# First chunk's mixing products in full fp32, W1 and W2 split later, and no identity products behind the first transposes

## What is computed

```python
t = rmsnorm(x, norm1_w)
xb = causal_depthwise_conv(t @ Wx, conv_w, conv_b)          # 4 taps along the sequence
r, i = sigmoid(xb @ Wa), sigmoid(xb @ Wi)
a = exp(-8 * softplus(lam) * r)
h = scan(a, sqrt(max(1 - a*a, 1e-12)) * (i * xb))            # h[s] = a[s] h[s-1] + b[s]
h1 = x + (h * gelu(t @ Wy)) @ Wo
u = rmsnorm(h1, norm2_w)
attn = h1 + (gelu(u @ Wg) * (u @ Wu)) @ Wd                   # Wg, Wu: 256 x 1024
x1 = layernorm(x + attn)
out = layernorm(x1 + relu(x1 @ W1 + b1) @ W2 + b2)           # W1: 256 x 1024
```

## Time and profile before

| | us |
|---|---|
| median of 3 runs | 622.78 (621.52 to 623.34) |
| the profiled execution | 621.15, of which the span is 619.4 |
| TensorE busy | 601.3 (97% of the span) |
| VectorE busy | 386.9 (62%) |
| ScalarE busy | 309.0 (50%) |
| GpSimd busy | 205.1 (33%) |

### The profile page before, as it was taken

The page is one execution under the profiler, slowest core; times in us unless marked ns, Lnnn a source line. Parts: engine busy times, 40 slices in busy tenths (PEclk is TensorE's granted clock), DMA queues, the critical chain, the costliest instruction groups (busy, mean ns, idle before and its releaser), DMA issues.

```text
span 619.4 us, 9569 instructions
## 1 busy us (share of the span) xinstructions
PE 601.3 (97%) x3681; PEld 536.6 (87%) x3681; DVE 386.9 (62%) x698; ACT 309.0 (50%) x580; POOL 205.1 (33%) x307
## 2 busy tenths in 40 slices
PE   7999988999999999999999999999999999999996
PEld 6897877789988898889888898888988898888996
DVE  5795676736585747747477465748467473663565
ACT  4865733365453754447444644537544473322353
POOL 5614137211724135130732216241451405241131
PEclk9999999999999999999999999999999999999999
DMA  8601001000100001010010101001000100000011
GB/s 274 228 2 34 1 2 35 0 1 2 34 1 1 34 1 36 2 34 1 1 35 2 34 1 35 0 1 35 2 1 1 35 1 1 1 19 18 0 35 35
DMA packets 13085, 15.69 MB, mean 25 GB/s; under 512 B 600, under 2 KB 12272, under 8 KB 13040
## 3 DMA queue, kind: packets, MB, share of 16 engines
q1 hardware_dynamic: 13040, 15.09, 7.2%
HBM read 10.89 MB, written 4.19 MB: 24 GB/s over the span
## 4 chain that ended last, share of the span: by engine, by line
PE 86%; DVE 8%; ACT 2%; POOL 2%; issue 1%; DMA 1%; POOLq 0%; DVEq 0%
PE psum L313 17%; PE psum L315 17%; PE psum L314 17%; PE psum L321 10%; PE psum L323 10%; PE psum L322 10%; PE psum L328 3%; DVE xb L847 1%; POOL normed L1218 1%; DVE row L922 1%; DVE xv L883 1%; DMA xs<-in_L_attn_x_dram 1%; PE psum L445 1%; PE psum L443 1%; PE psum L441 1%
## 5 line engine op out<-in xcount | busy, mean ns | idle before, releaser
L1247 POOL TENSOR_SCALAR gu_hi<-gu_raw 128x512 fp32r<-128x512 f32 x64 | 50.8, 794 | 318.3 <-DVE gu_raw L945 318.3
L955 DVE TENSOR_TENSOR hid_lo<-hid_raw,hid_hi 128x512 fp32r<-128x512 f32 x56 | 45.5, 813 | 83.9 <-ACT hid_hi L703 83.9
L699 ACT ACTIVATE hid_raw<-psum,vecs 128x512 f32<-128x512 f32 x56 | 38.4, 686 | 114.0 <-PE psum L315 114.0
L945 DVE TENSOR_TENSOR gu_raw<-psum,gu_raw 128x512 f32<-128x512 f32 x64 | 44.1, 689 | 81.3 <-PE psum L315 78.9
L321 PE MATMUL psum<-w_d_hi,gu_hi 128*128 128x256 f32 x256 | 72.8, 285 | 2.4 <-DVE gu_lo L950 2.4
L321 PE MATMUL psum<-w_hi,hid_hi 128*128 128x256 f32 x256 | 71.7, 280 | 0.6 <-DVE hid_lo L960 0.4
L323 PE MATMUL psum<-w_hi,hid_lo 128*128 128x256 f32 x256 | 71.8, 281 | 0.0
L323 PE MATMUL psum<-w_d_hi,gu_lo 128*128 128x256 f32 x256 | 71.8, 280 | 0.0
L322 PE MATMUL psum<-w_lo,hid_hi 128*128 128x256 f32 x256 | 71.7, 280 | 0.0
L322 PE MATMUL psum<-w_d_lo,gu_hi 128*128 128x256 f32 x256 | 71.6, 280 | 0.0
L690 ACT ACTIVATE gu_raw<-psum 128x512 f32<-128x512 f32 x64 | 38.1, 596 | 49.1 <-PE psum L315 48.4
(11 more groups left out here) (166 smaller groups left out, 1574.4 us busy)
## 6 DMA issues: line engine op xcount, KB each, us to landing
xs<-in_L_attn_x_dram SPq DMA_DIRECT2D x8, 512.0 KB, 3.5
out_dram<-row SPq DMA_DIRECT2D x15, 256.0 KB, 2.2
raw<-in_L_ffn_W_dram SPq DMA_DIRECT2D x2, 1024.0 KB, 13.0
raw_gud<-in_L_attn_Wg_dram SPq DMA_DIRECT2D x1, 1024.0 KB, 8.4
raw_gud<-in_L_attn_Wu_dram SPq DMA_DIRECT2D x1, 1024.0 KB, 10.5
raw_gud<-in_L_attn_Wd_dram SPq DMA_DIRECT2D x1, 1024.0 KB, 12.7
raw_xyai<-in_L_attn_Wx_dram SPq DMA_DIRECT2D x1, 256.0 KB, 2.8
raw_xyai<-in_L_attn_Wy_dram SPq DMA_DIRECT2D x1, 256.0 KB, 3.0
```

The source lines that it names most:

```text
L699: nc.scalar.activation(hid_raw[:, w % SLOTS, :], bank[:, :], ACT.Relu, bias=vec("b1", m)).then_inc(relu_ready, 1)
L945: nc.vector.tensor_tensor(gu_raw[:, r % SLOTS, :], up_bank(r)[:, :], gu_raw[:, r % SLOTS, :], ALU.mult).then_inc(gu_ready, 1)
L955: nc.vector.tensor_tensor(hid_lo[:, w % SLOTS, :], hid_raw[:, w % SLOTS, :], hid_hi[:, w % SLOTS, :].bitcast(FP32), ALU.subtract).then_inc ...
L1247: nc.gpsimd.tensor_scalar(gu_hi[:, r % SLOTS, :], gu_raw[:, r % SLOTS, :], 1.0, 0.0, ALU.mult, ALU.add).then_inc(gu_hi_ready, 1)
```

## The change

- The load of chunk 0's x is made in two halves, each with a semaphore. The square sums, the root, the scaling (now on VectorE) and the transposes of chunk 0 go by these pairs of row tiles.
- Chunk 0's products with Wx, Wa, Wi, Wy, Wo and chunk 1's with Wx and Wy are made in full fp32 from the raw weights and unsplit activations (`raw_step`, `raw_product`, `first_decay`, `first_out`). The norm weight, folded into the split Wx and Wy otherwise, is multiplied into `first_tT`. The order on TensorE is x, a, i of chunk 0, transposes of chunk 1, y of chunk 0, x of chunk 1, the output product, y of chunk 1.
- Chunk 1's products with Wa and Wi move from ahead of round 0 into round 3, its output product to round 6; the down product of round 7 moves ahead of the gate product of round 8.
- Wa, Wi, Wx, Wy and Wo are split in rounds 0 to 4 instead of ahead of round 0; W1 and W2 in rounds 8 and 9. Their loads are issued later, behind waits, since they lie over memory that other tiles use until then.
- The norm of h1 of chunks 0 and 1 goes by pairs, its scaling is on ScalarE (`first_norm_u`), and the transposes and splits of u go by pairs.
- Only the 8 identity products ahead of the transpose of the small vectors stay; the other 80 go.

The diff, cut to its core:

```diff
-            load_x(0)
+            for q in range(PAIRS):
+                load_first_x(q)
...
-            for n in ("x", "y", "a", "i"):
+            for n in ("x", "a", "i"):
                 load_w(n)
             load_x(1)
-            for n in ("g", "u", "o", "d", "1"):
+            for n in ("y", "g", "u", "o", "d"):
                 load_w(n)
             sync.dma_start(b2_rows[:, :], b2.partition_broadcast(P)).then_inc(b2_loaded, DMA)
+            sync.wait_ge(hi_split["d"], pieces["d"])
+            sync.wait_ge(lo_split["d"], pieces["d"])
             load_w("2")
...
+                if c == 2:
+                    sync.wait_ge(wy_done, 2 * KD)
+                    for n in ("x", "y", "a", "i"):
+                        sync.wait_ge(hi_split[n], pieces[n])
+                        sync.wait_ge(lo_split[n], pieces[n])
+                    load_w("1")
...
+            def raw_step(dst, n, m, k, moving):
+                return nc.tensor.matmul(dst, raw_weight(n)[:, k, m * P:(m + 1) * P], moving[:, k, :], start=(k == 0),
+                                        stop=(k == KD - 1))
...
+            def first_decay(bank):
+                for k in range(KD):
+                    pe.wait_ge(taps_added, taps_done(0, LOOKBACK - 1, k))
+                    for m in range(KD):
+                        last = raw_step(psum[bank + m][:, :], "a", m, k, xb)
...
-            nc.tensor.transpose(psum[GATE][:, 0:NV], vec_rows[:, :], ident[0:NV, 0:NV]).then_inc(vecs_transposed, 1)
-            keep_running(14, SECOND)
-            transpose_t(0)
-            keep_running(5, SECOND)
-            split_done("x")
-            mix_x(0)
-            split_done("y")
-            mix_y(0, bank=DOWN)
-            transpose_t(1)
-            keep_running(9, SECOND)
-            split_done("a", "i")
+            nc.tensor.transpose(psum[UP][:, 0:NV], vec_rows[:, :], ident[0:NV, 0:NV]).then_inc(vecs_transposed, 1)
+            transposed_by_pairs(normed, 0, t_ready, tT_done, MIX)
+            pe.wait_ge(w_loaded["x"], DMA)
+            first_x(0)
             pe.wait_ge(vecs_ready, 1)
-            mix_decay(0, bank=GATE)
-            mix_input(0, bank=SECOND)
-            mix_x(1)
+            pe.wait_ge(w_loaded["a"], DMA)
+            first_decay(GATE)
+            pe.wait_ge(w_loaded["i"], DMA)
+            raw_product(SECOND, "i", xb, wi_done)
+            pe.wait_ge(tap_done, 2)
+            pe.wait_ge(t_ready, 8)
+            transposed(normed, tT_done)
+            pe.wait_ge(w_loaded["y"], DMA)
+            raw_product(DOWN, "y", first_tT[0], wy_done)
+            first_x(1)
+            pe.wait_ge(w_loaded["o"], DMA)
+            pe.wait_ge(tanh_i_ready, KD)
+            first_out(SECOND)
             pe.wait_ge(gy_ready, KD)
-            mix_y(1, bank=DOWN)
-            pe.wait_ge(tanh_a_ready, KD)
-            keep_running(28, GATE)
-            split_done("o")
-            mix_out(0, bank=GATE)
-            pe.wait_ge(tanh_i_ready, KD)
-            keep_running(24, SECOND)
-            transpose_u(0)
-            mix_decay(1, bank=SECOND)
-            pe.wait_ge(gy_ready, 2 * KD)
-            mix_input(1, bank=DOWN)
-            split_done("g", "u")
+            raw_product(DOWN, "y", first_tT[1], wy_done)
+            transposed_by_pairs(normed, 0, u_ready, uT_done, GATE)
...
+                if r == KH:
+                    down(r - 1)
                 if units(r):
                     gate_up(r)
+                if r == 3:
+                    split_done("a", "i")
+                    mix_decay(1)
+                    mix_input(1)
...
+                if r == LAG_UP:
+                    act.wait_ge(lo_split["1"], pieces["1"])
+                    act.wait_ge(lo_split["2"], pieces["2"])
...
+                    if m == 3:
+                        tanh_decay(n)
                         exp_decay(n)
+                        tanh_input(n)
                         square_decay(n)
                         act.preload_act_table(ACT.Gelu_apprx_tanh)
-                    if m == 2:
+                    if m == 4:
                         gate_scale(n)
                         act.preload_act_table(ACT.Gelu_apprx_tanh)
+                        weight_hi("o")
...
+                if r == KH:
+                    weight_lo("1")
+                if r == KH + 1:
+                    weight_lo("2")
```

More of the change, by code:

```diff
@@ L56, in griffin_mlp_kernel @@
         raw_of = {}
+        with nc.sbuf_tensor("first_tT", [P, 2, KD, T], FP32) as raw:
+            first_tT = [raw[:, c, :, :] for c in range(2)]
         tT_hi = sb("tT_hi", [P, KD, T], FP32R)
@@ L60, in griffin_mlp_kernel @@
         mT_lo = sb("mT_lo", [P, KD, T], FP32R)
+        with nc.sbuf_tensor("raw_xyai", [P, 4, KD * D], FP32) as raw:
+            for at, n in enumerate("xyai"):
+                raw_of[n] = raw[:, at, :]
         with nc.sbuf_tensor("raw_1", [P, WIDTH], FP32) as raw:
@@ L330, in transposed, with transposed_by_pairs @@
                     last.then_inc(done, 1)
+            def transposed_by_pairs(src, c, ready, done, bank):
+                for q in range(PAIRS):
+                    pe.wait_ge(ready, 4 * c + 2 * q + 2)
+                    for tt in (2 * q, 2 * q + 1):
+                        for f in range(KD):
+                            last = nc.tensor.transpose(pair_bank(bank, q)[:, f, (tt % 2) * P:(tt % 2 + 1) * P],
+                                                       src[:, tt, f * P:(f + 1) * P], ident[:, :])
+                    last.then_inc(done, 1)
             def half_bank(bank, tt):
@@ L343, in transpose_t, with raw_weight, raw_product, first_x @@
             def transpose_t(c):
[L344 to L347, removed]
+                pe.wait_ge(uT_lo_ready, 2 * c)
                 pe.wait_ge(t_ready, 4 * c + 4)
                 transposed(normed, tT_done)
+            def raw_weight(n):
+                return raw_of[n].rearrange("p (k n) -> p k n", k=KD)
+            def raw_step(dst, n, m, k, moving):
+                return nc.tensor.matmul(dst, raw_weight(n)[:, k, m * P:(m + 1) * P], moving[:, k, :], start=(k == 0),
+                                        stop=(k == KD - 1))
+            def raw_product(bank, n, moving, done):
+                for m in range(KD):
+                    for k in range(KD):
+                        last = raw_step(psum[bank + m][:, :], n, m, k, moving)
+                    last.then_inc(done, 1)
+            def first_x(c):
+                pe.wait_ge(first_tT_ready, 4 + 2 * c)
+                raw_product(MIX, "x", first_tT[c], wx_done)
+            def first_decay(bank):
+                for k in range(KD):
+                    pe.wait_ge(taps_added, taps_done(0, LOOKBACK - 1, k))
+                    for m in range(KD):
+                        last = raw_step(psum[bank + m][:, :], "a", m, k, xb)
+                        if k == KD - 1:
+                            last.then_inc(wa_done, 1)
+            def first_out(bank):
+                for q in range(PAIRS):
+                    for k in range(KD):
+                        if q == 0:
+                            pe.wait_ge(hy_ready, k + 1)
+                        for tt in (2 * q, 2 * q + 1):
+                            last = nc.tensor.matmul(half_bank(bank, tt), gy[:, k, toks(tt)], raw_weight("o")[:, k, :],
+                                                    start=k == 0 and tt % 2 == 0, stop=k == KD - 1,
+                                                    skip_group_check=True)
+                    last.then_inc(wo_done, 1)
             def mix_x(c):
-                pe.wait_ge(tT_lo_ready, 2 * c + 2)
+                pe.wait_ge(tT_lo_ready, 2 * (c - 2) + 2)
                 for m in range(KD):
@@ L552, in round_of @@
                     mix_y(n)
-                if mixing and m == 5:
+                if mixing and m == 5 and p >= 1:
                     mix_out(n)
@@ L614, in split_hi, with split_hi_by_pairs @@
                     nc.scalar.activation(dst[:, f, :], psum[MIX + f][:, :], ACT.Copy).then_inc(ready, 1)
+            def split_hi_by_pairs(dst, c, bank, done, ready):
+                for q in range(PAIRS):
+                    act.wait_ge(done, 2 * c + q + 1)
+                    nc.scalar.activation(dst[:, :, half(q)], pair_bank(bank, q), ACT.Copy).then_inc(ready, 1)
             def conv_start(c, m):
@@ L774, in round_of @@
                         hy_hi(n)
-                if mixing:
+                if mixing and p >= 1:
                     if m == 7:
```

355 lines of the change are left out of this document (226 added, 129 removed).

## The result

The changed kernel takes 625.13 us (median of 20 runs, 624.05 to 627.04), the kernel before 622.75 (20 runs, 621.52 to 624.51): ratio 1.0041, 95% interval 1.0031 to 1.0050. The forecast was 619.8. The time lies within the range, but on the other side: 2.4 us slower instead of 3.0 faster. The profiled execution took 625.44 us with a span of 623.6, 4.2 more than the profiled span of before. The medians differ by less, since the profiled execution of before, 621.15, is quicker than all these 20.

A forecast was written before the change was run, and what follows sets the result against it. TensorE holds 86% of the chain; the gain is how much earlier `mlp_up(0)` begins. Round 0 at 43.0 plus 47.4 gives 90.4, plus 23.2 gives 113.6 against 116.52: about 3.0 us, 619.8 from the median; range 613.5 to 626.

The forecast's parts named there:

- they stand in waits: TensorE's identity products: they were claimed to be worth nothing in themselves.
- the first product: `first_x(0)` on TensorE, at the start: forecast to begin at 8.6 us, against 13.33 before.
- the term of rounds 0 to 7: From round 0's gate product to round 8: 42.5 us of work plus 4.9 of waits, 47.4 in all.
- hidden: Split of Wi, round 3: ends just as it is due, with no cover; each us more is a us of end.
- the rival in which full fp32 is cheap: Full fp32 at 0.46 us a product; with VectorE alone with Wg, G is 36, time 613; chance 0.25 shared with clock staying up.
- Rounds 8 to 10: Round 8 to `mlp_up(0)`: W1 and W2 splits on VectorE lengthen 18.92 us by 4.3 to 23.2.
- The cover of the loads: W1 and W2 loads, issued later on SP: both there by 75 us, used from 95, so costing nothing.
- round 0 at 43.60 (43.0 forecast): Gate product of round 0 (G): forecast at 43.0 us, after VectorE's halves of Wg, Wu and `uT_lo`.
- The rival that came true: Clock falls again where identity products ran: 5.3 us lost in two places, 625.1 us; chance 0.20.
- Its test: At the start of round 0: this rival decides if TensorE's granted clock is then at its lower level.
- Its reason against: Ahead of 94.93 us: a 2.19 us wait left round 8 at its usual pace.
- its two places: Gap after 13.8 us (`first_decay` at half clock, 3.5 us) and 39.4 to 43 (gate and up pair, 2.7).

## Why the prediction was wrong

**The step that failed.** The prediction put the identity products at nothing ("they stand in waits") and gave the waits of the changed kernel a loss of clock in one place only, the first product. With those waits filled the kernel is 4.5 us quicker; some 1.9 of it are at the first product (5.51 us against 3.63), which the forecast had at the lower clock, and the rest is what it left out. The forecast has 5.2 us for it, from 8.6 to 13.8, the first half at the lower clock; that is the author's estimate and no run shows such a half: the 8 instructions took 5.51 us from 9.77 on, at a recorded 1.00. The second step is in the term of rounds 0 to 7: the split of Wi was "hidden", and TensorE waited 2.04 us for it. The miss is larger than the medians tell. Against the profiled executions the forecast was a span of 616.4 and the measured one is 623.6, 7.2 more; the 619.8 from the median took over the 1.6 us by which the median of before lies above its profiled execution.

**The balance.** With the waits filled, the kernel before takes 621.6 us, the changed one 620.7, and the changed one with W1 and W2 split early 616.4. So at the full clock the late splitting costs 4.3 us and the rest of the change brings 5.2; the unfilled waits cost the changed kernel 4.5 and give 625.1. Against the real median of before, 622.8, that is 5.2 + 1.2 gained less 4.3 and 4.5: 2.4 us slower.

**Right.** A full fp32 product of 512 columns is two instructions 0.43 us apart in the changed kernel (6.87/16, from the row at 25.72 to the one at 32.59): dearer than three split ones, 2.76/4 = 0.69. The 0.87 us for such a product and the 0.43 for one of 256 columns in the forecast's sum are shown by no run of the kernel before; the changed kernel showed 0.86 (6.87/8) and 0.43 (32.59 to 36.04, 3.45/8), and not the 0.46 of the rival in which full fp32 is cheap. The waits of 2.50 ahead of the down product of round 5 (2.5) and 1.52 ahead of the output product (1.7). Rounds 8 to 10: 119.34 - 96.22 = 23.12 (23.2), with a wait of 5.22 (some 5) behind VectorE's gate times up. The price of the late splitting, 18.9 to 23.2, is confirmed by the kernel with it undone, 4.3 us. The cover of the loads held: no wait of the changed kernel was for W1 or W2 to land.

**Right by luck: round 0 at 43.60 (43.0 forecast).** `first_x(0)` began at 9.77 and not near 8.6, and `first_decay` at 17.44. What set the end was not VectorE either. I had priced two halves of Wg at 2.1 us each, beside GpSimd's splitting of Wd (in the kernel before they took 4.19 beside its splitting of Wg and Wu, 22.65 to 29.5, and not of Wd). That came later, and both halves took 2.48 us together; it was GpSimd that was slow in that time, 1.62 us for the root of the second pair instead of 0.70 (no run takes them apart). The scaling, the transposes and ScalarE's `uT_hi` followed it, and VectorE waited for them (GpSimd's timeline, then VectorE's, changed kernel):

```profile
36.51 0.70 POOL L1370 TENSOR_TENSOR rstd<-rstd,minus_half 128x2 f32<-128x2 f32 x1
...
38.92 1.62 POOL L1370 TENSOR_TENSOR rstd<-rstd,minus_half 128x2 f32<-128x2 f32 x1
```

```profile
37.51 2.48 DVE L1150 SCALAR_TENSOR_TENSOR w_g_lo<-raw_gud,vecs,w_g_hi 128x1024 fp32r<-128x1024 f32 x2
...
42.00 0.69 DVE L986 TENSOR_TENSOR uT_lo<-psum,uT_hi 128x512 fp32r<-128x512 f32 x1 [0.82 <-ACT uT_hi L717]
```

**Wrong: rounds 0 to 7, 52.62 us instead of 47.4.** Three things are in it. (1) The clock in round 0: from 43.60 to the gate product of round 1 at 48.05 are 4.45 us, against 2.76 for a pair, 1.7 lost. (2) Wi in round 3: "hidden, but with no cover" was the right warning and the wrong value. I priced the splits by rows taken alone, and GpSimd's addition made two of them 1.77 and 1.76 instead of 0.69: 2.0 us of wait. (3) Another 1.5 us, of which 1.0 lies at the last transposes of u: 0.45 us idle ahead of them, and 1.43 from their start to the next product (93.28 to 94.71) where I took 0.9. ScalarE makes the square sums of chunk 2's x (1.6 us) before the gelu of round 7 and the scaling of `first_norm_u(1)`, and I had left them out of its queue; the scaling began only at 92.34. This third one is read from the trace only; I didn't try another order. Together 5.2, plus 0.6 at the start: from 3.0 us of gain to 2.8 of loss at `mlp_up(0)`.

**Wrong: the clock behind the wait that I foresaw.** I forecast 5 us of idle ahead of `mlp_up(0)` and didn't ask what clock comes after. The products behind it ran at 0.55: the span grew by 4.2 us, of which 2.8 are there at `mlp_up(0)`, so this cost 1.4 more; filling that wait gave 1.8.

**The rival that came true.** "The clock falls again where identity products ran", 625.1, held 0.20. Its test, the granted clock as round 0 begins, came out nearly as it says: 1.00 up to 44.0, 0.50 from 44.5 on. Its reason against, that 2.19 us of wait ahead of 94.93 had left no mark, rested on one execution, and the steps in the runs of before show that others lose time. It should have had more than half: the end of the kernel showed a fall after some 2.2 us of rest, and the forecast has several waits of 1.7 to 5 us with one drop of clock in all. The price showed in the kernel before without its 80 identity products: 7.7 us.

The time of 625.1 that the rival gave is right by luck. Of its two places only the second had the drop: the products of `first_decay`, behind 2.17 us of wait, ran at about the pace of the full clock (4 instructions in 1.95 us, 12 with those of Wi in 5.42; recorded 1.00 from 17 to 24). The drop behind 5.22 us ahead of `mlp_up(0)` and the 2 us of Wi stood in none of my cases.

The chances have a slip too: six tenths of 0.40, with 0.25 and 0.10, are 0.59 and not 0.56.

## What to carry to other kernels

Products that nobody reads are not free to remove from a wait (7.7 us for the 80 of the kernel before): price each wait that TensorE is left with, old or new, with the loss of clock that may lie behind it, some 1.4 to 1.8 us in the changed kernel, and check the granted clock in several executions and not in one. Filling one wait can bring nothing while others stay open (625.19 against 625.13 with 10 identities ahead of round 0). When work is put off, ask what stands behind it on the same engine at the new place: four halves of W1 and W2 were idle-time work in rounds 0 to 7 and 4.3 us of critical path in rounds 8 to 10. Before an operation that gives a semaphore is moved, follow the DMA queue behind that semaphore too.

## What the runs showed of the hardware

Behind some waits of TensorE the granted clock was 0.50, behind others of like length 1.00, and which wait it was differed between kernels. The changed kernel's profile had a drop to 0.50 behind the waits of 1.11 and 1.41, from 44.2 to 47.6 us, and none (1.00) behind those of 2.04 and 2.50; with 10 identities ahead of round 0 the drop stood behind the wait of 2.07 in round 3 (0.65 from 62 to 66). Nor were the drops of one length: 3.4 us there, and with the addition moved 0.50 in all of 80 to 86. What decides it stays open.

The granted clock as recorded doesn't always fit the pace of the products. At 8 to 16 us of the changed kernel it reads

```profile
8.00:16.00 8.00, 6.13 (x11) 2.39 (x10) 3.41 (x14) 2.24 (x5) 0.00 (x0) 1.00 1.01 383
```

while the 8 instructions from 9.77 took 5.51 us against 3.63 at 9.89 in the kernel filled at the start. TensorE had no idle time within either group. At the beginning of a kernel I would go by the distance between like instructions. That the clock made the difference here is not shown.

Some instructions of VectorE and GpSimd took longer beside each other than I had priced. VectorE's split of Wa took 1.76 us beside GpSimd's addition of two tensors and 0.69 with that addition moved away. GpSimd's root for two tiles took 0.70 us at 36.51 and 1.62 at 38.92, while VectorE split the halves of Wg; no run takes those two apart.
